# Local attention on one core: the slots of all stages moved

## The reference

```python
for i in range(DEPTH):        # DEPTH = 6
    x = attn_layer(shift_tokens(x), Wqkv[i], q_scale[i], k_scale[i], Wo[i]) + x
    x = ffn_layer(shift_tokens(x), ln_g[i], ln_b[i], W1[i], b1[i], W2[i], b2[i]) + x
```

## Time and profile before

| | |
|---|---|
| median of 3 runs | 4757.02 us (4753.99 to 4761.74) |
| profiled execution, its own time | 4742.66 us |
| its span, first to last instruction | 4740.9 us |
| mean granted TensorE clock | 0.966 |
| phase B, by its marks | about 577 to 3989 us of the span |

### The profile page before, as it was taken

The page is one execution under the profiler, slowest core; times in us unless marked ns, Lnnn a source line. Parts: engine busy times, 40 slices in busy tenths (PEclk is TensorE's granted clock), DMA queues, the critical chain, the costliest instruction groups (busy, mean ns, idle before and its releaser), DMA issues. The chain is left out here.

```text
span 4740.9 us, 124337 instructions
## 1 busy us (share of the span) xinstructions
PE 4207.0 (89%) x45166; PEld 3132.2 (66%) x45166; DVE 4008.7 (85%) x7658; ACT 3751.7 (79%) x11543; POOL 3521.7 (74%) x2504
## 2 busy tenths in 40 slices
PE   6988699999999999999999999999899997688887
PEld 3555477777777777777777777777777775445453
DVE  4676798989988889889889899888998895598887
ACT  1555588888888888888888888888888886777774
POOL 0010699999999889988999999999899894444444
PEclk8999799999999999999999999999999998788888
DMA  1000111112111121111111111111111111000000
GB/s 26 7 6 2 47 51 39 45 40 57 52 40 45 43 54 50 42 44 45 52 46 45 43 47 51 47 45 40 50 51 41 45 39 31 0 4 3 3 3 5
DMA packets 118569, 168.67 MB, mean 36 GB/s; under 512 B 26563, under 2 KB 44422, under 8 KB 118022
## 3 DMA queue, kind: packets, MB, share of 16 engines
q1 hardware_dynamic: 109246, 160.92, 12.8%
q10 hardware_dynamic: 8776, 0.45, 0.1%
HBM read 20.79 MB, written 2.10 MB: 5 GB/s over the span
## 5 line engine op out<-in xcount | busy, mean ns | idle before, releaser
L1380 POOL TENSOR_TENSOR b_w<-b_w,b_vt 128x512 f32<-128x512 f32 x768 | 1190.5, 1561 | 273.7 <-DVE b_ss L1295 143.2
L1384 POOL TENSOR_TENSOR b_rn<-b_ssm,all_neg_half 128x16 f32<-128x16 f32 x384 | 1174.9, 3060 | 32.0
L1177 ACT ACTIVATE b_Pr<-ps,b_nm 128x96 f32<-128x96 f32 x3072 | 1002.6, 353 | 0.6
L1177 ACT ACTIVATION_READ_ACCUMULATOR b_Pr<-ps,b_nm 128x1 f32 x3072 | 676.0, 220 | 0.0
L1220 ACT ACTIVATE b_PT<-ps 96x512 f32<-96x512 f32 x768 | 456.8, 595 | 259.7 <-PE ps L1029 246.6
L992 PE MATMUL ps<-all_ident,b_w 128*128 128x128 f32 x3072 | 454.7, 278 | 175.4 <-DVE b_xtok L282 109.0
L1063 PE MATMUL ps<-b_Whi,b_xlo 128*128 128x512 f32 x1152 | 572.3, 497 | 34.5 <-DVE b_vt L1293 19.5
L1343 DVE TENSOR_TENSOR b_Pr<-b_Pr,b_rinv 128x384 f32<-128x384 f32 x768 | 541.7, 705 | 26.3
L1029 PE MATMUL ps<-all_ident,b_Pr 128*96 128x128 f32 x3072 | 475.7, 277 | 62.8 <-ACT b_PT L1220 45.2
L1291 DVE TENSOR_TENSOR b_w<-ps,until_b_rotab 128x512 f32<-128x512 f32 x768 | 523.5, 682 | 8.9 <-ACT b_sq L1197 4.8
L1293 DVE TENSOR_TENSOR b_vt<-ps,until_b_rotab 128x512 f32<-128x512 f32 x768 | 521.8, 679 | 0.0
(11 more groups left out here) (259 smaller groups left out, 9365.4 us busy)
## 6 DMA issues: line engine op xcount, KB each, us to landing
b_V<-b_Vraw SPq DMA_DIRECT2D x384, 192.0 KB, 2.6
b_V<-b_Vraw SPq DMA_DIRECT2D x384, 128.0 KB, 2.4
b_V<-b_Vraw SPq DMA_DIRECT2D x192, 64.0 KB, 2.2
b_Wraw<-in_L_ffn_Wqkv SPq DMA_DIRECT2D x36, 256.0 KB, 3.3
b_Wo<-in_L_ffn_Wo SPq DMA_DIRECT2D x6, 512.0 KB, 4.2
a_xtok<-in_L_attn_hidden_states SPq DMA_DIRECT2D x16, 128.0 KB, 2.1
out<-c_xout SPq DMA_DIRECT2D x16, 128.0 KB, 1.8
b_W<-in_L_ffn_W SPq DMA_DIRECT2D x6, 341.0 KB, 3.5
```

What stands on the lines that cost most here:

```text
L1177: last = nc.scalar.activation(s.Pr[:, r % 2, j, i], ps[:, S_BANK[j], i * KEYS:(i + 1) * KEYS], ACT.Exp, bias=s.nm[:, r, j, i:i + 1], accum ...
L1380: nc.gpsimd.tensor_tensor(rows, rows, s.vt[:, i % 4], ALU.add).then_inc(s.pool_add, 1)
L1384: nc.gpsimd.tensor_tensor(s.rn[:, j], s.ssm[:, j], g.neg_half[:, 0:HB], ALU.pow).then_inc(s.pool_r, 1)
```

## The change

Only slot constants change. The order of GpSimd's pieces stays the same; that of the other three engines changes in places: piece 0 moves behind the scores of round 0, the first half of the output product before the scores of round 1, the late normalisation (j = 3) before rotation 0, the scale of each round one to two slots sooner, the split between the two scales of round 0, the statistics before the scale of round 2, the transposes of q and k into another order, and W2's product behind round 2's values.

```diff
-QK_SLOT = {0: (0, 0), 2: (0, 2), 6: (1, 0), 8: (1, 2), 16: (0, 1), 17: (0, 3), 22: (1, 1), 24: (1, 3)}
-V_SLOT = {15: (0, 4), 21: (1, 4), 29: (0, 5), 30: (1, 5)}
+QK_SLOT = {1: (0, 0), 2: (0, 2), 5: (1, 0), 6: (1, 2), 15: (0, 1), 18: (0, 3), 23: (1, 1), 24: (1, 3)}
+V_SLOT = {14: (0, 4), 21: (1, 4), 29: (0, 5), 30: (1, 5)}
...
-LATE_SLOT = {0: (0, 3), 4: (0, 1), 6: (1, 3), 7: (1, 1)}
-WO_SLOT = (11, 12)
-W1_SLOT = {5: 0, 17: 2, 21: 1}
-XT_SLOT, XN_SLOT, W2_SLOT = 21, 31, 29
-TRANSPOSE_SLOT = {22: (0, 0), 26: (1, 2), 27: (1, 0), 28: (0, 2)}
+LATE_SLOT = {0: (0, 3), 4: (0, 1), 6: (1, 1), 10: (1, 3)}
+WO_SLOT = (7, 12)
+W1_SLOT = {4: 0, 18: 1, 19: 2}
+XT_SLOT, XN_SLOT, W2_SLOT = 20, 31, 29
+TRANSPOSE_SLOT = {23: (1, 2), 25: (0, 2), 26: (1, 0), 27: (0, 0)}
 READ_LAG = 0
 
-SCORE_LAG, EXP_LAG, SCALE_LAG, TURN_LAG, VALUE_LAG, COPY_LAG = 0, (4, 5), (7, 8), (8, 11), 14, 15
-
-RES_SLOT, STATS_SLOT, END_SLOT, SPLIT_SLOT = 14, 24, 31, 8
-DVE_NORM_SLOT = {27: 2}
-DVE_LATE_NORM_SLOT = {4: 3}
-POOL_NORM_SLOT = {7: 0, 16: 1}
-GELU_SLOT, RSTD_SLOT, GATE_SLOT = 21, 23, 19
+SCORE_LAG, EXP_LAG, SCALE_LAG, TURN_LAG, VALUE_LAG, COPY_LAG = 0, (4, 5), (5, 7), (8, 10), 13, 15
+
+RES_SLOT, STATS_SLOT, END_SLOT, SPLIT_SLOT = 13, 21, 28, 5
+DVE_NORM_SLOT = {28: 2}
+DVE_LATE_NORM_SLOT = {1: 3}
+POOL_NORM_SLOT = {5: 0, 16: 1}
+GELU_SLOT, RSTD_SLOT, GATE_SLOT = 21, 23, 22
```

## The result

The changed kernel takes 4908.1 us (median of 4, 4902.2 to 4914.8), the kernel before 4755.5 in the same four rounds (4750.5 to 4761.7): +152.6 us, a ratio of 1.0322 [1.0308, 1.0336]. Slower, as forecast, but by 153 us instead of 105, and 3 us outside the range. The profiled execution took 4914.8 us, 4913.0 of them its span. That is 172 us more than the profiled execution of the kernel before (which is faster than all its timed runs here), and 166 of these lie in phase B: from the first to the last L1266 it is 3576.9 us, for 3411.2 in the earlier trace rows.

The account below looks back on a forecast made before the run. No single engine but a loop through several bounds a pair of steps (71.57 us). Terms of +2.25 and about +0.1 give +2.35 us a pair, 105 us over 48 pairs, so 4757 + 105 = 4862 us; range 4745 to 4905.

Parts of the forecast that it names:

- Totals, waits, tie: Local attention: no engine stands out, nobody waits for nearly full GpSimd; it ties with VectorE at the GELU step's start.
- (1) Statistics: Statistics before round 2's scale, transposes later: TensorE's stalls of 1.20 us (B) and 1.16 us (A, with the GELU) go.
- (2) The loop: Late normalisation before rotation 0 closes power, normalisation, rotation, addition into a loop: 2.6 us of idle GpSimd each step.
- (3) Piece 0: Projection piece 0 behind round 0's scores delays rotation 0; GpSimd's add 0 starts 4.9 us after the scores' start, not 3.3.
- (4) contention: VectorE's normalisation falls into GpSimd's pause, so GpSimd's round shortens by 0.8 us, between 0 and 1.26.
- From A's piece 2 to B's S today 32.48: From the GELU step's (A) piece 2 to the next step's (B) round 0 scores (S): 32.48 us, ScalarE-led, nearly unchanged.
- R1: Rival, faster: TensorE's freed stalls decide the pair of steps; -18 us, 4739 us; chance 0.20.
- R2: Rival, no change: GpSimd's own loop decides and contention falls 1.2 us a round; 4757 us; chance 0.10.
- R3: Rival, slower by less: only the normalisation loop counts, TensorE and ScalarE absorb piece 0; +0.8 to +1.2 a pair, 4800; chance 0.15.
- R4: Rival, slower by more: END's wait on VectorE is uncovered, next scores 1.15 us later; 4912 us; chance 0.05.

Follow-up runs that it names:

- e14: The kernel before, with only the last GpSimd power of a step (j = 3) replaced by a multiplication: 4754.2 us, 1.0011.
- e13: The changed kernel, with only the last GpSimd power of a step (j = 3) replaced by a multiplication: 4760.9 us, 1.0027.
- e7: The kernel before, with only the statistics moved ahead of the scale of round 2: 4739.3 us, 0.9996.
- e4: The changed kernel, with piece 0 put back ahead of the scores of round 0: 4893.2 us, 1.0326.
- e2: The kernel before, with only the late normalisation (j = 3) moved ahead of rotation 0: 4803.2 us, 1.0131.
- e6: The kernel before, with only piece 0 moved behind the scores of round 0: 4847.9 us, 1.0218.
- e9: The changed kernel itself, timed again beside other runs on the same chip: 4908.1 us, 1.0352.
- e1: The changed kernel, with the late normalisation (j = 3) put back behind rotation 1: 4801.0 us, 1.0127.
- e8: The changed kernel, with the late normalisation back behind rotation 1 and piece 0 back ahead of the scores: 4745.9 us, 1.0009.
- e12: The changed kernel, with late normalisation and piece 0 both put back and the GELU two slots later: 4747.1 us, 1.0009.
- e15: The changed kernel, with the late normalisation placed between rotation 0 and rotation 1: 4944.0 us, 1.0424.
- e5: The changed kernel, with 9 unused matmuls added on TensorE before piece 2 in every odd step: 4861.2 us, 1.0253.
- e3: The changed kernel, with 18 unused matmuls added on TensorE before piece 2 in every odd step: 4913.6 us, 1.0365.
- e10: The changed kernel, with GpSimd's power replaced by a multiplication for all four tile pairs: 4908.1 us, 1.0349.

## Why the prediction was right in direction and too small

**Totals, waits, tie.** Right. GpSimd and VectorE met without slack at A's start, and e14 shows with e13 that GpSimd's power was on nobody's path before and is on TensorE's after.

**(1) Statistics.** Right that the stall at L282 goes and that B gets shorter (33.53 against 34.66); e7 shows that the stall was worth nothing alone. In A the stall didn't go; another releaser took its place: the transposes that waited 1.16 us for L282 and then 0.56 for L1147 now wait 2.14 for L1147.

**(2) The loop.** Right, with its terms: 2.54 us of GpSimd's idle time for 2.6. It is paid in each pair's A, and also in B, where GpSimd idles 4.0 us before add 0 (2.46 before) without TensorE waiting for it.

**(3) Piece 0, (4) contention.** The two come out in one number, the start of A's piece 2 behind B's S: 40.92 us, for 41.35 forecast. Add 0 starts 4.77 behind B's S, for 4.9. The contention's saving was a little larger than the 0.8 taken and nowhere near 0: GpSimd's round from B's add 0 takes 33.61 us for 34.69. Add 1 is down to 1.27; the split comes only behind it, and the product of the scale that now lies beside it pays on VectorE (L1343, 1.65 us for 0.56 alone). Whether piece 0 has a price of its own next to the loop isn't settled (e4: nothing to 0.5%), and the sum of separate prices would be no measure of it: 1.3% for L1302 (e2) and 2.2% for piece 0 (e6) make 3.5%, which is just what the changed kernel costs on that chip (e9), but that is luck: in the changed order they are worth 3.2% and 1.2%, and overlap (e1, e4, e8).

**The step that failed** is the term "From A's piece 2 to B's S today 32.48", carried over as 32.6. It measured 34.32. Of the 1.7 us missing, 1.47 lie between piece 2 and the scores of round 1 (6.60 against 5.13 in B of the same kernel): the work there was priced at the clock of the earlier trace rows, 1.00, though my own sum had made a stall of over 2 us on TensorE in front of it. Some 0.2 us more lie in the new order between piece 2 and round 2, and the rest of the stretch, from round 2 to B's S, took 20.42 us for 20.35 forecast. In the sum: 0.43 less, 1.72 more, so 1.29 a pair over the forecast's 73.9, and with the prediction's 44 effective pairs 57 us. That is most of the 67 us by which the profiled execution (4914.8) lies above the forecast for it (4848). Against the medians only 46 us are missing; that part is luck, since the two profiled executions lie 172 us apart and the medians 153. The mean pair gives 3.43 x 48 = 165 us, the 166 of phase B. The stall was foreseen and its echo wasn't. Before, the phase had stalls of up to 1.8 us at a clock of 1.00, so no row there showed this cost; the new stall was to be longer than any of those, and the upper bound should have held a second price for it: the products behind it at the lower of the two clock levels. That the clock would fall there couldn't be known from the rows, only that it might.

**R1** fell by e7 and by the loop (its sum also adds 0.87 where 0.77 was worked out, so that -18 us should have been -24; it decides nothing). **R2**'s condition nearly came, 1.08 us of contention saved in B's round for its 1.2, and the pair is 75.2 all the same: the loop runs through VectorE and TensorE, and GpSimd's own sum doesn't decide. **R3** was near in that piece 0's place adds little to the loop (e4), and wrong in that TensorE doesn't take the loop's stall in: 3.4 us a pair for its 0.8 to 1.2. **R4** gave the nearest number (4912) for the wrong reason: its wait is there (40.9 us in 26 places) and e8 shows that it costs nothing.

No kernel here beats the one before: e7 (0.9996), e8 and e12 (1.0009) can't be told from it.

## What to carry to other kernels

Before an instruction is moved ahead in an in-order queue, close the loop: what it waits for, what stands behind it, and whether its releaser waits for that; the idle time is the sum round the loop, and a place half way (e15) doesn't cut it. Give a stall of some 2 us that the change makes on TensorE two prices: its length, and as an upper bound the work behind it at the lower clock, which here came behind some such stalls and not behind others. Prices of single moves in such a schedule don't add: measure the pair, and expect a "removed" cost to let other work slide onto something worse.

## What the runs showed of the hardware

- Behind a TensorE stall of 2.16 us the granted clock was 0.50 for about 3 us (1.2 GHz), which made the work between piece 2 and round 1 1.5 us longer. Where that stall was filled or removed (e5, e8, e1), the clock fell behind the one of 2.14 us at the GELU, 20 to 27 times in some 27 pairs; in e13, with the same stall at the GELU, it fell 5 times. e8 has 27 falls and takes 1.0009 of the time of the kernel before, which has none. That fits with the half of the step that ScalarE leads, where these falls lie, but no run here takes them out alone.
- VectorE's instructions were stretched by GpSimd's far more than the earlier trace rows had shown in the other direction: L1248 0.42 to 2.03 us, L1245 0.29 to 1.98, L1302 1.21 to 2.29, L1343 0.56 to 1.65. The Trainium skill (GPSIMD Engine Reference, Specifications) says that GpSimd shares its SBUF interfaces with VectorE; these rows agree, and the sizes are this case's.
- 18 matmuls of 128 columns in fp32 left 36 records and took 4.18 us, 0.23 us each (e3).
- GpSimd's power of 128x16 in fp32 took 2.93 us and more; a multiplication of the same shape 0.31 us in the mean (e10).
